# The first cross-attention's eight value-output weight folds moved into the state-space loop and written over the output weights

## The reference, cut to what matters

```
x = x + L0_attn(layernorm(x))          # a state-space mixer (512 channels, state 16)
x = x + L0_xattn(layernorm(x), ctx)    # 16 heads of 128
# L0_xattn:
q = rmsnorm((h @ Wq) by head);  k = rmsnorm((ctx @ Wk) by head);  v = (ctx @ Wv) by head
out = softmax(q k^T / sqrt(128)) v;    return out.reshape(B, S, 16*128) @ Wo
```

## Time and profile before

| | |
|---|---|
| median of 3 runs | 925.9 us (923.86 to 926.99) |
| the profiled execution | 924.2 us, span 922.3 us, mean granted PE clock 0.963 |
| busy in the span | PE 822.4, DVE 549.7, ACT 433.7, POOL 302.3 us |
| share of the chain that ended last | PE 56%, ACT 11%, DVE 11%, DMA 9%, POOL 7%, issue 6% |

### The profile page before, as it was taken

The page is one execution under the profiler, slowest core; times in us unless marked ns, Lnnn a source line. Parts: engine busy times, 40 slices in busy tenths (PEclk is TensorE's granted clock), DMA queues, the critical chain, the costliest instruction groups (busy, mean ns, idle before and its releaser), DMA issues.

```text
span 922.3 us, 12515 instructions
## 1 busy us (share of the span) xinstructions
PE 822.4 (89%) x5082; PEld 502.2 (54%) x5082; DVE 549.7 (60%) x666; ACT 433.7 (47%) x650; POOL 302.3 (33%) x148
## 2 busy tenths in 40 slices
PE   6797897986989889999999899998989799989977
PEld 2232342332445456666666676666677466657755
DVE  3799989899895223333424534347792534565686
ACT  2774566545433555555564321233654222232475
POOL 0089999899880000000001001111017993000000
PEclk9889899899899999999999999999999999999999
DMA  9576666656994200000000121405100000000001
GB/s 309 149 190 175 179 163 179 185 173 173 246 229 154 108 1 1 1 1 1 1 1 12 41 92 64 177 18 192 69 3 1 1 1 1 1 1 1 1 1 46
DMA packets 26376, 77.02 MB, mean 84 GB/s; under 512 B 3568, under 2 KB 10480, under 8 KB 25072
## 3 DMA queue, kind: packets, MB, share of 16 engines
q1 hardware_dynamic: 25552, 74.13, 27.4%
q0 software_dynamic: 768, 2.10, 0.7%
HBM read 68.75 MB, written 7.08 MB: 82 GB/s over the span
## 4 chain that ended last, share of the span: by engine, by line
PE 56%; ACT 11%; DVE 11%; DMA 9%; POOL 7%; issue 6%; SPq 0%; POOLq 0%; DVEq 0%; ACTq 0%
PE ps L1297 11%; PE ps L1213 9%; DMA region_b<-m_rows 5%; POOL region_c L468 4%; PE ps L1396 4%; PE ps L1422 4%; PE ps L1285 4%; PE ps L1260 4%; DMA region_c<-m_rows 3%; PE ps L1218 2%; PE ps L1095 2%; PE ps L1047 2%; POOL region_b L468 2%; PE ps L1166 2%; PE ps L1465 2%
## 5 line engine op out<-in xcount | busy, mean ns | idle before, releaser
L1213 PE MATMUL ps<-xnT,region_a 128*128 128x512 f32 x256 | 120.1, 599 | 1.4 <-ACT region_c L718 0.8
L468 POOL TENSOR_TENSOR region_c<-region_c,region_b 128x1024 f32<-128x1024 f32 x42 | 100.9, 2410 | 54.6 <-DMA region_b<-m_rows 47.5
L1095 PE MATMUL ps<-region_c,ident 128*128 128x512 f32 x168 | 90.0, 665 | 17.2 <-POOL region_c L468 11.0
L1874 DVE TENSOR_TENSOR_SCAN region_c<-region_c,ps 128x1024 f32<-128x1024 f32 x43 | 97.9, 2283 | 1.7 <-ACT ps L643 0.4
L489 POOL DMA_INDIRECT f_in<-xn,f_row x8 | 8.0, 995 | 277.2 <-DVE f_row L1985 275.4
L1951 DVE COPY region_b<-ps 128x512 f32<-128x512 f32 x32 | 21.4, 689 | 83.7 <-PE ps L1271 83.6
L1213 PEld LDWEIGHTS ps<-xnT,region_a 128*128 128x128 f32 x256 | 47.2, 190 | 41.2 <-issue 35.8
L1869 DVE TENSOR_TENSOR ps<-ps,region_c 128x1024 f32<-128x1024 f32 x52 | 63.3, 1217 | 10.3 <-PE ps L1083 10.3
L1095 PEld LDWEIGHTS ps<-region_c,ident 128*128 128x128 f32 x168 | 34.2, 212 | 58.0 <-issue 33.6
L1297 PE MATMUL ps<-region_c 128*128 128x256 f32 x256 | 59.8, 380 | 0.0
L1297 PEld LDWEIGHTS ps<-region_c 128*128 128x128 f32 x256 | 48.5, 190 | 16.7 <-issue 11.5
(11 more groups left out here) (252 smaller groups left out, 1636.3 us busy)
## 6 DMA issues: line engine op xcount, KB each, us to landing
region_b<-m_rows SPq DMA_DIRECT2D x43, 512.0 KB, 5.1
region_c<-m_rows SPq DMA_DIRECT2D x21, 512.0 KB, 5.1
xn<-m_brows SPq DMA_DIRECT2D x12, 512.0 KB, 4.3
region_a<-in_x_wo SPq DMA_DIRECT2D x2, 2048.0 KB, 10.9
m_rows<-region_b SPq DMA_DIRECT2D x4, 512.0 KB, 5.5
region_a<-in_x_wq SPq DMA_DIRECT2D x8, 256.0 KB, 7.2
region_b<-in_f_fc SPq DMA_DIRECT2D x1, 2048.0 KB, 7.9
region_b<-in_f_proj SPq DMA_DIRECT2D x1, 2048.0 KB, 13.1
```

What stands on the lines that cost most here:

```text
L468: pool.tensor_tensor(m_hc[u % 3], m_h[u % 3], m_cb[u % 3], ALU.mult).then_inc(sem("m_hc"), 1)
L1095: last = pe.matmul(ps[:, 4 + c, :], ident[:, :], m_hc[u % 3][:, c * HALF:c * HALF + HALF], start=(n == 0), stop=(n == DST - 1))
L1213: last = pe.matmul(b, w, xnT[:, k, cols(it)], start=(k == 0), stop=(k == KH - 1))
L1874: dve.tensor_tensor_scan(m_h[u % 3], m_da[u % 3].rearrange("p b t -> p (b t)"), inputs(u), 0.0, ALU.mult, ALU.add).then_inc(sem("m_scan"), 1)
```

## The change

1. The eight folds leave iterations 0 and 1 of `cross(0)` (PE's `fold`, ACT's `folded`, and their places in `head_order`).
2. They are made in the loop: `loop_fold(i)` on PE behind the other work of steps n = 7 to 10 of blocks 0 and 2 (fold 0 to 3 and 4 to 7), in banks 6 and 7 in turn; from the third of each block on PE waits until ACT has copied the fold of two before. ACT's `loop_folded(i)` copies one step later, n = 8 to 11. PE's wait for ACT's copy of the C rows moves from n = 11 to n = 7 there, and at n = 11 PE waits for the block's folds to be copied.
3. The results are written over `wo` (two heads' result over those two heads' output weights): `wvo[0]` is now A 32 to 48 KB.
4. `wvT` is loaded in two halves: heads 0 to 7 at the start into `ctxn`'s tile, in place of `ctxn`; heads 8 to 15 by SP at step 0 of the loop, into A 28 to 32 KB, ahead of that step's `m_bb` and `m_cb`. `ctxn` itself is loaded at step 4 of block 1, behind a wait for the first four folds. The 1 MB load after the loop is gone.
5. The feed-forward's sorted rows and their transposes (`f_rows`, `f_xT`) move to C 0 to 15 KB, where `wvo[0]` was.
6. The semaphores `x1_fold` and `x1_folded` of the second cross-attention's early folds become `w_fold` and `w_folded`, with counts eight higher.

```diff
-        wvT = view("A", 24, [NH, CD])
+        wvT = [ctxn[:, :, :], view("A", 28, [NH // 2, CD])]
-        wvo = [view("C", 0, [NH, D]), view("A", 24, [NH, D])]
+        wvo = [view("A", 32, [NH, D]), view("A", 24, [NH, D])]
-        f_rows = view("A", 24, [SORTED, D])
-        f_xT = [view("A", 29 + 5 * i, [SORTED, KH, 128]) for i in range(2)]
+        f_rows = view("C", 0, [SORTED, D])
+        f_xT = [view("C", 5 + 5 * i, [SORTED, KH, 128]) for i in range(2)]
+        X0_FOLDS = NH // 2
...
                         if layer == 0:
                             order += [(("k", it, a), "act")]
-                            if it < 2:
-                                order += [(("wvo", 4 * it + a, 0), "act")]
...
-            load(ctxn[:, :, :], io["ctxn"], "ld_x0")
+            load(wvT[0], io["x0_wvT"][:, 0:NH // 2, :], "ld_x0")
...
                     if j == 0:
                         sp.wait_ge(sem("st_brows"), 16)
+                        load(wvT[1], io["x0_wvT"][:, NH // 2:NH, :], "ld_x0")
...
+                if k == 1 and n == 4:
+                    sp.wait_ge(sem("w_folded"), X0_FOLDS // 2)
+                    load(ctxn[:, :, :], io["ctxn"], "ld_xqk")
...
-            load(wvT, io["x0_wvT"], "ld_x0")
...
+            def loop_folded(i):
+                act.wait_ge(sem("w_fold"), i + 1)
+                act.activation(fold_out(0, "wvo", i), ps[:, 6 + i % 2, :], ACT.Copy).then_inc(sem("w_folded"), 1)
...
+                    if n in (8, 9, 10, 11) and k != 1:
+                        loop_folded(X0_FOLDS // 2 * (k // 2) + n - 8)
...
-                            if it < 2:
-                                folded(4 * it + a)
...
+            def fold_wvo(layer, i, b):
+                for a in range(2):
+                    h = 2 * i + a
+                    wv = wvT[h // (NH // 2)][:, h % (NH // 2), :] if layer == 0 else wvT1[:, h // 2, :]
+                    last = pe.matmul(b[:, 256 * a:256 * a + 256], wv, (wo, wo1)[layer][:, h, :],
+                                     start=True, stop=True)
+                return last
+
+            def loop_fold(i):
+                if i == 0:
+                    pe.wait_ge(sem("ld_x0"), 64)
+                if i % 4 >= 2:
+                    pe.wait_ge(sem("w_folded"), i - 1)
+                fold_wvo(0, i, ps[:, 6 + i % 2, :]).then_inc(sem("w_fold"), 1)
...
+                    if n in (7, 8, 9, 10) and k != 1:
+                        if n == 7:
+                            pe.wait_ge(sem("m_cT"), k + 2)
+                        loop_fold(X0_FOLDS // 2 * (k // 2) + n - 7)
                     if n == 11:
                         if k != 1:
-                            pe.wait_ge(sem("m_cT"), k + 2)
+                            pe.wait_ge(sem("w_folded"), X0_FOLDS // 2 * (k // 2) + 4)
                         convolve(k + 1)
...
-                                if it < 2:
-                                    fold(4 * it + a)
...
-            pe.wait_ge(sem("ld_xqk"), 192)
+            pe.wait_ge(sem("ld_xqk"), 208)
```

More of the change, by code:

```diff
@@ L550, in norm_rows, with fold_out @@
                     ln_turned(ln, g)
+            def fold_out(layer, what, i):
+                if what == "wvo":
+                    return wvo[layer][:, 2 * i:2 * i + 2, :].rearrange("p a n -> p (a n)")
+                return wqk[:, 2 * i:2 * i + 2].rearrange("p a b c -> p (a b c)")
+            def loop_folded(i):
+                act.wait_ge(sem("w_fold"), i + 1)
+                act.activation(fold_out(0, "wvo", i), ps[:, 6 + i % 2, :], ACT.Copy).then_inc(sem("w_folded"), 1)
             def exp_tables():
@@ L1159, in _ @@
                     ln_turn(1, 1)
-            def fold_wvo(layer, i, b):
-                wv_h, wo_h = (wvT, wo) if layer == 0 else (wvT1, wo1)
-                for a in range(2):
-                    h = 2 * i + a
-                    last = pe.matmul(b[:, 256 * a:256 * a + 256], wv_h[:, h if layer == 0 else h // 2, :],
-                                     wo_h[:, h, :], start=True, stop=True)
-                return last
             def fold_wqk(i, b):
@@ L1533, in early_fold @@
                     last = fold_wqk(i, ps[:, 6 + m % 2, :])
-                last.then_inc(sem("x1_fold"), 1)
+                last.then_inc(sem("w_fold"), 1)
             def a_turn_rows(half):
```

16 lines of the change are left out of this document (6 added, 10 removed).

## The result

The median is 914.75 us (910.07 to 919.38, nine runs) against 924.92 us (921.55 to 928.2, nine runs of the kernel before beside them). The ratio is 0.9901, 95% interval 0.9882 to 0.9919: 9.2 us less, between 7.5 and 10.9 (the medians themselves lie 10.2 us apart; the ratio is the one on record, and the 9.2 us are worked out from it). Forecast were 7.5 us less and a median of 918.4 us. The lines of `after` have other numbers: L1230 is the queries' line (L1213 before), L1235 the keys' (L1218), L719 the copy of the queries' bank (L711), L470 POOL's product (L468), L1889 and L1884 DVE's scan and product (L1874, L1869), L1116 `add_state`, L1089 `put_b`, L654 the copy of the shared product (L643).

The account below looks back on a forecast made before the run. POOL was taken to pace the loop, and PE's waits for ACT to empty banks the attention's iterations 0 and 1. Terms: -9.4 + 2.0 - 0.1 = -7.5 us, 925.9 to 918.4 us, range 914.5 to 922.5.

Parts of the forecast that it names:

- the load at the start: Step 0: the new 512 KB ahead of POOL's first product costs 2.0 us; rival that it is hidden, chance 0.12.
- The attention: Iterations 0 and 1 of `cross(0)`: without folds the next queries take the freed bank sooner, 9.4 us saved.
- The folds in the loop at nothing: Blocks 0 and 2: eight folds and copies are hidden, 0 us; rival that they make it slower, 933 us, chance 0.05.
- Step 8: Loop: ACT's shared-product copy ends 0.3 us before DVE's scan; rival of small loop costs (here or late C transfer), chance 0.12.
- `ctxn` in block 1 at nothing: Step 4 of block 1: 512 KB more where POOL never waits for a DMA, costed at nothing, at most 2 us.
- The 1 MB after the loop gone, -0.1: End of the loop: DVE's 0.52 us wait for the last C rows may shrink, gain 0 to 0.5, taken as 0.1 us.
- Blocks 1 and 2 still at 60.8: Loop: expected sign that blocks 1 and 2 still last 60.8 us, equal with and without folds.
- signs of being wrong: Block 0 or 2 over 1 us longer, POOL waiting for DMA in block 1, or clock below 1.0 before iteration 2.
- The clock in the attention: Rival: idle PE without folds lowers the clock, two heads cost 1.9 us more each, 922.2 us; chance 0.05.

Follow-up runs that it names:

- the repetition: The changed kernel unaltered, run again for more runs and a second profile: 914.65 us, ratio 0.9887 to the kernel before.
- the late half: The changed kernel with the second half of `wvT` loaded at step 7 of block 1 instead of step 0: 916.48 us, ratio 0.9927.
- the old loads: The changed kernel with its loop folds kept but all loads as in the kernel before: 914.14 us, ratio 0.9884.
- the filler: The kernel before plus four unread fold-sized products on PE at steps 7 to 10 of blocks 0 and 2: 928.33 us, ratio 1.0025.

## Why the prediction was right, step by step

The mechanism was right where the gain is. The number was a narrow hit: 914.75 us lies 0.25 us inside the range of 914.5 to 922.5, and of the repetition's interval (8.2 to 12.8 us less) the forecast's 7.5 is outside. The one term that is shown to be mis-sized is the load at the start.

- *The attention*: forecast 9.4 us, 9.48 in the profiles, and the same window in the kernel without folds. It holds by heads too: heads 0 and 2 gave 0.98 us each as forecast, head 1 1.54 and 1.91 (forecast 1.4 and 1.9), and head 3 with what follows it 1.05 and 1.06 (forecast 1.1). The chain of banks is shown by the folds in other banks (6.1 us without less work) and by the keys in other banks (4.2 us more).
- *The folds in the loop at nothing*: right. Taking them out gained nothing, and three times the folds cost 0.65 us in block 2. (PE's share was given as 3.5 us for four folds at the pace of 0.98 us each; that is 3.9, and changes nothing.) The reason that I gave was right as well: blocks 1 and 2 of the earlier trace rows had the same low stretch of the clock (0.57 for 4 us, at 11 to 15 us of one and 12 to 16 of the other), so that their comparison was a fair one. I did not know that when I made it.
- *Step 8*: "it fits, by a little" was wrong, though not through ACT. DVE waited 1.12 us there, because POOL's shared product came late behind C rows that came late, most likely by the new load; I had costed the load at POOL's first product and not looked at its second wait. If so, it is part of the load's price.
- *The load at the start*: the term that was mis-sized. Forecast 2.0 us, bounds 0 to 3.4. Block 0 is 57.90 us on average in the six profiles without it (58.24, 57.70, 58.00, 57.78, 58.00, 57.67) and 59.05 in the seven with it (59.24, 58.92, 58.45, 58.19, 59.87, 59.36, 59.31): about 1.2 us. The kernel with three loads more is left out of this. Counted from the first issue to POOL's first product, it is 7.57 us on average in the six without the load (6.40 to 8.27) and 8.51 in the seven with it (8.44 to 8.80): 0.9 us. More of them cost 1.4 us each. Averages over single profiles, with 57.67 to 58.24 and 58.19 to 59.87 as ends, are no more than that: in whole times neither the late half nor the old loads made after faster. Six of the seven profiles with the load also have the folds, and the one without them has 58.19; that the load costs more beside the folds is not excluded. I had taken 1.9 us from landings of transfers that were also issued 0.4 us apart, and that difference of issue should have been taken off. By the Trainium skill ("DMA: Bandwidth & Descriptors", section "Bandwidth") 512 KB take, as an estimate, 1.5 us at 358 GB/s; the runs agree with the rule better than with my rows, and their 1.2 and 1.4 us lie a little under it.
- *`ctxn` in block 1 at nothing*: right; POOL waited for no DMA in that block in after.
- *The 1 MB after the loop gone, -0.1*: DVE's wait for the last C rows is 0.44 us instead of 0.52, and the stretch from block 3 to the first query is 0.10 us shorter. That is the forecast's figure, but the same stretch lies between 66.8 and 71.0 us in the fourteen profiles, so that it proves little.
- *Blocks 1 and 2 still at 60.8*: wrong as a test. The lengths 61.62 and 59.11 broke it by 0.8 and 1.7 us in both directions, for the reason above and not through the change. Two more of the signs of being wrong that I had set were met or nearly so, while the forecast held: block 0 is longer by just 1.00 us (0.68 in the repetition), and the clock fell below 1.0 before iteration 2 in the repetition.
- *The clock in the attention*: the rival had 0.05 and 3.8 us. In after's first profile the clock is 1.00 throughout, but in its repetition and five other profiles of kernels with heads of 3.25 us the clock falls for about 4 us with the scores of iteration 0, and the window is 43.84 to 43.89 us instead of 42.34. So it comes, costs 1.5 us, and not where I looked for it. The filler's kernel, whose attention still has its folds, has it at the same place (53.32 us instead of 51.82), so it isn't only the missing folds that bring it. The other two profiles of kernels with such heads don't have it. The Trainium skill ("TensorE: Matmul & The Clock Gate", section "A second HAM failure mode: psum-queue depth-cycling") would have it fall from the banks' cycle; between the heads, where that cycle is, it stayed at 1.00 in after.

With the load at its measured size the sum is -9.5 + 1.2 - 0.1 = -8.4 us, inside the interval of -7.5 to -10.9 and at the edge of the repetition's, -8.2 to -12.8. What remains to the centres is 0.8 and 2.1 us. It is not explained. Two things could hold it and were not told apart: the start ahead of the loop, 1.5 to 3.1 us shorter in both profiles of after than in the eleven profiles with a slow start, and the clock in the loop's blocks.

## What to carry to other kernels

Where jobs take turns in two PSUM banks, count the jobs in the chain, not the matmuls: a job moved out gives back most of the hand-over, even when PE still does it next door in an idle bank (6.1 of 9.5 us in the window, in spite of a low clock at its end). The cheapest version that was run gives the folds banks 0 and 1 and touches neither the loop nor the loads; the best moves the folds to the loop and the keys to other banks. The keys alone in other banks were not run. Before reading a difference of 1 to 3 us between two profiles as an effect, compare the granted clock of the same stretch in both; two blocks are comparable only where it agrees.

## What the runs showed of the hardware

- The length of a 60 us block moved in three levels (59.1, 60.3 to 60.8, 61.6 to 62.3 us) with the granted clock of one stretch of 4 to 8 us, in executions of the same program too (59.11 and 60.80 us for block 2 of after).
- A higher mean clock is not a shorter time: the filler raised the clock of a 20 us window from 0.91 to 1.00 and the kernel was 2.3 us slower, though the mean clock of its runs was higher too (0.967 against 0.963). Yet between executions of one program the two go together. A line through the 139 runs whose clock is on record, with a level of its own for each kernel, gives 0.61 us less for each 0.001 of mean granted clock; what is left has a standard deviation of 1.4 us.
- The first matmuls of an execution can run at half speed: weight loads 0.86 us apart instead of 0.43, up to about 19 us, which put 3.1 us on the profiled execution of before. Eleven of fourteen profiles have such a start, 1.5 to 3.1 us longer than the other three. The granted clock of that stretch is given as 1.00 in both traces, so the time of the instructions has to be read there, not the clock column.
- Three more 512 KB loads' worth of data in front of a queue of such loads delayed POOL's first product by 4.1 us, 1.4 us each. Block 0 kept all of it to its end.
